# Moving the second chunk's recurrence into the next step, with shorter blocks and a new order, in an RWKV attention and feed-forward kernel

## What is computed

```python
xx = shift(x) - x;  lo = tanh((x + xx * maa_x) @ maa_w1.T) @ maa_w2      # four mixes
xrg, xwa, xk, xv = x + xx * (lo + time_maa)
r = xrg @ Wr.T;  k = xk @ Wk.T;  v = xv @ Wv.T;  g = tanh(xrg @ gate_w1.T) @ gate_w2
w = -softplus(-(time_decay + tanh(xwa @ decay_w1.T) @ decay_w2)) - 0.5
...                                    # kk (normalised), a, ma, mk, k, b = -kk * a
def step(s, inp):                      # per head, 32 x 32 state
    q_, w_, k_, v_, a_, b_ = inp
    sa = s @ a_
    s = s * exp(-exp(w_)) + outer(sa, b_) + outer(v_, k_)
    return s, s @ q_
y = head_norm(y) * ln_w + ln_b + rk * v
x = x + (y * g) @ Wo.T
x = x + quantised_matmul(layernorm(x), weight_q) + bias
```

## Time and profile before

| | before |
|---|---|
| median of three runs | 3132.63 us |
| the profiled execution | 3138.99 us, its span 3137.3 us |
| TensorE busy | 2873.8 us, 92% |
| VectorE busy | 2807.0 us, 89% |
| ScalarE busy | 1672.6 us, 53% |
| GpSimd busy | 1420.0 us, 45% |

### The profile page before, as it was taken

One profiled execution on the slowest core, in us unless ns is written; L12 is line 12 of the kernel. 1 busy time (PEld: TensorE's weight loads), 2 busy tenths in 40 slices (PEclk: granted clock), 3 DMA queues, 4 the chain that ended last, 5 costly groups with the idle time before them and its releaser, 6 DMA issues.

```text
span 3137.3 us, 175510 instructions
## 1 busy us (share of the span) xinstructions
PE 2873.8 (92%) x80064; PEld 2523.7 (80%) x80128; DVE 2807.0 (89%) x5699; ACT 1672.6 (53%) x3334; POOL 1420.0 (45%) x1224
## 2 busy tenths in 40 slices
PE   5899999999999999999999999999999999999995
PEld 5788788888887887888888888888888888888874
DVE  4898899999999998999999999999999899889985
ACT  3464555555554654655655655555555545546552
POOL 5344444444444444444444444444444444444442
PEclk9999999999999999999999999999999999999997
DMA  4121221222222222212212212212222222222121
GB/s 132 40 64 40 57 53 45 64 50 49 62 50 47 64 50 47 64 44 54 64 43 55 64 43 55 56 45 60 53 48 61 50 47 64 50 48 64 42 49 39
DMA packets 92603, 170.68 MB, mean 54 GB/s; under 512 B 13908, under 2 KB 14932, under 8 KB 91864
## 3 DMA queue, kind: packets, MB, share of 16 engines
q1 hardware_dynamic: 91864, 159.45, 21.7%
HBM read 41.97 MB, written 16.78 MB: 19 GB/s over the span
## 4 chain that ended last, share of the span: by engine, by line
PE 87%; DVE 7%; issue 5%; SPq 1%; DMA 0%; ACT 0%; POOL 0%; POOLq 0%; ACTq 0%; DVEq 0%
PE bank L1100 31%; PE bank_a L1239 12%; PE bank L1300 8%; PE bank L1107 4%; PE bank_a L1217 4%; PE bank_b L1217 4%; DVE stacked L939 4%; PE bank_a L1270 3%; PE bank_b L1270 3%; PE bank_a L1247 3%; PE bank_a L1255 3%; PE bank_b L1290 2%; PE bank_a L1290 2%; PE bank L1182 2%; DVE xm_k L816 2%
## 5 line engine op out<-in xcount | busy, mean ns | idle before, releaser
L1239 PE MATMUL bank_a<-pw,w_ffn_int 32*32 32x64 f32 x16384 | 273.0, 216 | 37.9 <-issue 33.2
L420 POOL TENSOR_TENSOR xm_wa<-xm_wa,xT 128x512 f32<-128x512 f32 x64 | 75.4, 1178 | 500.4 <-DVE xm_wa L816 500.4
L1239 PEld LDWEIGHTS bank_a<-pw,w_ffn_int 32*32 32x32 f32 x16384 | 242.3, 105 | 66.3 <-issue 53.2
L1100 PE MATMUL bank<-xm_rg,w_r 128*128 128x128 f32 x2048 | 285.7, 282 | 3.1 <-issue 3.1
L1100 PE MATMUL bank<-xm_v,w_v 128*128 128x128 f32 x2048 | 269.1, 279 | 4.6 <-issue 3.1
L527 ACT ACTIVATE pw<-bank_a 128x512 f32<-128x512 f32 x192 | 114.6, 597 | 287.2 <-PE bank_a L1239 286.7
L1100 PEld LDWEIGHTS bank<-xm_rg,w_r 128*128 128x128 f32 x2048 | 249.9, 192 | 15.4 <-issue 3.9
L1300 PE MATMUL bank<-w_o,yc 128*128 128x512 f32 x512 | 251.2, 614 | 11.3 <-DVE yc L781 10.3
L1100 PEld LDWEIGHTS bank<-xm_v,w_v 128*128 128x128 f32 x2048 | 245.1, 192 | 13.5 <-issue 7.7
L1100 PE MATMUL bank<-xm_k,w_k 128*128 128x128 f32 x2048 | 240.8, 276 | 2.0 <-issue 2.0
L1100 PEld LDWEIGHTS bank<-xm_k,w_k 128*128 128x128 f32 x2048 | 235.5, 193 | 2.2 <-issue 2.2
(11 more groups left out here) (198 smaller groups left out, 8334.3 us busy)
## 6 DMA issues: line engine op xcount, KB each, us to landing
streamed<-aq_state SPq DMA_DIRECT2D x128, 384.0 KB, 5.3
streamed<-w_ffn_int SPq DMA_DIRECT2D x128, 384.0 KB, 5.3
xin<-in_x SPq DMA_DIRECT2D x128, 128.0 KB, 4.8
xres<-in_x SPq DMA_DIRECT2D x128, 128.0 KB
out<-o_sb SPq DMA_DIRECT2D x128, 128.0 KB, 2.4
w_ffn_int<-in_weight_q SPq DMA_DIRECT2D x1, 2048.0 KB, 9.7
w_k<-in_Wk SPq DMA_DIRECT2D x1, 1024.0 KB
w_r<-in_Wr SPq DMA_DIRECT2D x1, 1024.0 KB
```

What stands on the lines that cost most here:

```text
L420: return nc.gpsimd.tensor_tensor(out_, in0, in1, ALU.add)
L1100: ins = mm(bank[:, o * n:(o + 1) * n], weights[:, k, o * P:(o + 1) * P], x[:, k].rearrange("p b t -> p (b t)"), start=(k == 0), stop=(k == ...
L1239: ins = mm(bank_a[q, 64 * n:64 * n + 64], pt[q, g, :], source[q, g, 0:2].rearrange("p j t -> p (j t)"), start=True, stop=True)
```

## The change

Four things change, and no matmul is added or removed.

The second chunk's from_values_and_state, solve_step, from_solutions, right_hand_sides, update_state, solution and outputs are called in the finish part of the next step, for tile n. Both chunks now use bank_b, so scores_k waits until both outputs of the tile before are read, and scores_b waits only for the inverse of the tile before. As scores_b of tile m is masked before chunk 1 of tile n is done, `first` becomes [P, 6, G, CHUNK], with two sets of the parts that from_solutions reads.

VectorE's and GpSimd's functions with several operations are split into functions with one (key_norm into squares_turned, squares_summed and squares_floored, and so on), and these are placed apart in tile_step.

VectorE's second product in scores_b (the crossing block) becomes an activation of ScalarE with mask_half as its scale, and VectorE's product for tx in half_inverse (the corner block) two activations. ScalarE's copy of the queries to r_raw goes: VectorE's queries_decayed reads the bank itself. gn_rstd is now yc's space in place of rn's.

All four orders of tile_step (TensorE, VectorE, ScalarE, GpSimd) are new; SP's stays.

```diff
+            def crossing(m):                                   # ScalarE
+                act.wait_ge(v_pm, count(m, 1, 1))
+                act.wait_ge(v_sums, count(m, POWERS, 0))
+                run(first[:, 1, :, 0:HALF], pairs(bank_a)[:, :, 0, HALF:], ACT.Identity,
+                    scale=mask_half[:, 0:1]).then_inc(a_e, 1)
+            def inverse_blocks(m):
+                act.wait_ge(v_t4, count(m, 1, 1))
+                act.wait_ge(p_u, count(m, NC, 0))
+                for a in range(2):
+                    c = slice(a * HALF, (a + 1) * HALF)
+                    ins = run(tx[:, :, c], pw[:, :, 1, HALF:], ACT.Identity, scale=mask_half[:, a * HALF:a * HALF + 1])
+                ins.then_inc(a_tx, 1)
...
-                dve.wait_ge(a_r, count(i, 1, 1))
-                tt(aq[:, 1], r_raw[:], pdec[:, :, 1:], ALU.mult).then_inc(v_q, 1)
+                tt(aq[:, 1], by_chunk(fb[2]), pdec[:, :, 1:], ALU.mult).then_inc(v_q, 1)
...
             def scores_b(m):                                   # TensorE
-                pe.wait_ge(a_y, count(m, NC, 0))
+                pe.wait_ge(v_t, count(m, 1, 0))
             def scores_k(m):
+                pe.wait_ge(a_y, count(m, NC, 0))
             def from_values_and_state(m, c):
-                bank = step_bank(c)
+                bank = bank_b
                 if c == 1:
-                    pe.wait_ge(v_t, count(m, 1, 1))
+                    pe.wait_ge(a_y, count(m, NC, 1))
```

More of the change, by code:

```diff
@@ L702, in tile_step @@
                     removal_pairs(m)
+                    key_pairs(m)
                 if project:
                     keys(i)
-                if solve:
-                    key_pairs(m)
+                if finish:
+                    solution(n, 1)
+                if project:
+                    a_gate(i)
+                    mk_gate(i)
+                if solve:
+                    crossing(m)
+                if project:
+                    decay_gate(i)
+                if finish:
+                    outputs(n, 1)
+                if project:
+                    ma_gate(i)
                 if finish:
                     squared_heads(n)
-                if project:
-                    a_gate(i)
-                    ma_gate(i)
-                if solve:
-                    value_pairs(m)
-                if project:
-                    mk_gate(i)
-                    squares(i)
                 if solve:
@@ L1284, in from_solutions @@
             def from_solutions(m, c):
-                bank = step_bank(c)
+                bank = bank_b
+                own = 2 + 2 * (m % 2)
                 if c == 0:
@@ L1322, in tile_step @@
                     keys(i, [0, 1])
+                if finish:
+                    from_values_and_state(n, 1)
+                if project:
                     keys(i, [2, 3])
+                if finish:
+                    solve_step(n, 1)
                 if solve:
@@ L1327, in tile_step @@
                     gates(i)
[L1328 to L1329 removed]
+                if finish:
+                    from_solutions(n, 1)
                 if project:
@@ L1340, in tile_step @@
                 if project:
-                    queries(i, [1])
-                    values(i, [2])
+                    values(i, [3])
+                if solve:
+                    scores_k(m)
+                if project:
                     queries(i, [2])
+                    queries(i, [3])
+                if solve:
+                    power(m, 2)
                 if mix:
@@ L1346, in tile_step @@
                 if solve:
-                    power(m, 2)
-                if project:
-                    queries(i, [3])
-                    values(i, [3])
+                    output_gate(m)
                 if finish:
@@ L1359, in tile_step @@
                 if solve:
-                    from_values_and_state(m, 0)
-                    inverse(m)
+                    half_inverse(m)
+                if project:
+                    gate_hidden(i)
                 if mix:
                     low_rank(j)
-                if project:
-                    gate_hidden(i)
                 if solve:
-                    solve_step(m, 0)
-                    output_gate(m)
-                    from_solutions(m, 0)
+                    from_values_and_state(m, 0)
                 if mix:
@@ L1372, in tile_step @@
                 if solve:
-                    from_values_and_state(m, 1)
-                if finish:
-                    quantised(n)
-                if solve:
-                    solve_step(m, 1)
-                if finish:
-                    feed_forward(n)
+                    inverse(m)
+                    solve_step(m, 0)
                 if mix:
@@ L1382, in tile_step @@
                 if solve:
-                    from_solutions(m, 1)
+                    from_solutions(m, 0)
+                if finish:
+                    quantised(n)
                 if mix:
                     hidden(j, 1)
+                if finish:
+                    feed_forward(n)
             pe.wait_ge(const_done, 1)
```

311 lines of the change are left out of this document (192 added, 119 removed).

## The result

The changed kernel is slower: 3259.39 us median (3247.39 to 3270.24) against 3135.11 us of the kernel before, run beside it; the ratio is 1.0384 [1.0358, 1.041]. The forecast was 3089 us with a range up to 3158. The profiled execution of after took 3247.39 us.

The account below looks back on a forecast made before the run. TensorE, with its waits, was taken to bound the 47.4 us step; -1.35 + 1.2 - 0.5 = -0.65 us a step, times 63 is -41, with the start -44: forecast 3089 us, range 3040 to 3158.

Parts of the forecast that it names:

- Second chunk's waits, -1.35: TensorE's waits at chunk 1's from_values_and_state, solve_step and feed_forward would go, covered by other matmuls: -1.35 us a step.
- Issue gaps elsewhere, -0.5: TensorE's unexplained stops in power and half_inverse would shrink as long matmul groups move apart: -0.5 us a step.
- The new wait, +1.2: solve_step(m,0) would wait +1.6 us a step for VectorE's xm_wa, xm_k, inverse; hidden issue gaps make it +1.2 net.
- the sign that the prediction had named: The prediction would be wrong if solve_step(m,0) waited over 2 us; 1.0 to 1.6 us was expected.
- a slack of 1.4 us: Time VectorE would have in hand each step to reach xm_wa before TensorE has filled the banks of mixed_inputs.
- 0.41 of issue gaps: The inverse's own issue gaps on TensorE, 0.41 us a step, would be free inside solve_step's new wait.
- Rival 3: VectorE late at xm_wa, lengthening solve_step(m,0)'s wait; decides from 0.65 us of lateness; slower, about 3183 us; chance 0.23.
- VectorE, 43.9 to 41.5: VectorE's work per step would fall from 43.9 to 41.5 us, by blocks leaving it and by splitting.
- The other 1.2, from the splitting: Separating about twelve dependent pairs of VectorE operations, gap about 0.1 us each, would save 1.2 us a step.

Follow-up runs that it names:

- norm_late: Changed kernel with only VectorE's second_norm and row_maximum moved behind inverse(m): 3182.5 us, ratio 1.0114 to the kernel before.
- gate_between: norm_late plus VectorE's inverse(m) between xm_wa and xm_k, ScalarE's value_pairs behind the table load, TensorE's gate_hidden(i) between inverse(m) and solve_step(m,0): 3100.88 us, ratio 0.9845.
- before_wait: Kernel before the change, with only VectorE's inverse(m) moved behind the quantiser so that solve_step(m,0) waits: 3215.35 us, ratio 1.0244.

## Why the prediction was wrong

*Second chunk's waits, -1.35.* Right. The waits of from_values_and_state, feed_forward and solve_step for rhs_sb fell from 86.2 us to about 4 (the last three rows of the list of waits): -1.28 a step.

*Issue gaps elsewhere, -0.5.* Right in size. The waits of before that answer to the list of after:

```profile
PE bank_a L1239 <- issue: 35.2, 48, 2.3
PE bank_a L1247 <- issue: 25.6, 37, 1.6
...
PE bank L1100 <- issue: 15.7, 18, 2.0
```

The issue gaps of power and half_inverse fell from 60.8 us to 23.3, which is -0.59; against it those of the projections rose from 15.7 to 24.0, +0.13. (The 63.7 of the prediction is all idle time of two rows and holds some waits for VectorE too.) That the spacing did it is argued from the order and wasn't tried alone.

*The new wait, +1.2.* This step failed first, and by the sign that the prediction had named: solve_step(m,0) waits over 2 us (2.13). The chain xm_wa, xm_k, inverse was read rightly: without the 0.58 us of lateness the wait in the step shown would be 1.33. But the sum took VectorE to be on time, on a slack of 1.4 us that wasn't there, and netted 0.41 of issue gaps that didn't shrink (36.2 us now). Wait and gaps of the inverse are 2.7 us a step together, where I had 1.6: 1.1 us too little. Rival 3 named the mechanism (VectorE late at xm_wa, by collisions with GpSimd and ScalarE's row ahead of power) and the point from which it decides, 0.65 us; by wait and gaps the lateness that reached TensorE was about 1.1 us. second_norm's stretch is 0.83 us of VectorE's delay ahead of xm_wa, its wait for GpSimd's rs another 0.43. I gave that rival 0.23 and 3183 us. Where the slack went stands in VectorE's own waits in after:

```profile
DVE rhs_sb L991 <- PE bank_b L1387: 92.5, 61, 1.9
DVE first L812 <- PE bank_a L1334: 86.5, 64, 2.0
DVE w_ffn_int L968 <- ACT pw L540: 85.9, 79, 4.3
...
DVE x2n L1055 <- POOL rs L477: 28.4, 63, 0.8
```

The prediction counted about 1 us a step each at scores_b's mask (L812) and at power(m,2) (L968, all three powers); they are 1.35 and 1.34. The waits at right_hand_sides (1.45) and for GpSimd's rs (0.44) it didn't count.

*VectorE, 43.9 to 41.5.* Wrong. Its busy time is 43.6 us a step. The crossing and the corner block did leave it (-1.22), but second_norm and scaled_rows took 0.83 and 0.50 more, and the small operation that makes `shift`, in norm_shift, 0.47 (172 to 644 ns each). The other 1.2, from the splitting, was too much to begin with: the earlier trace rows give 0.06 to 0.08 us a pair, not 0.1, and part of that is a gap, which busy time doesn't hold. That operations collide was right, but the earlier trace rows were misread: GpSimd's operation of 2.43 us starts 0.75 us behind values_centred and isn't the one that stretches it. A product of 1.31 us is, which starts at 1498.15, 0.50 us ahead: it runs on for 0.81 us, and values_centred takes 0.67 longer than its best. So the row speaks for a hold until the product ends, not against it. I didn't look for which operations would newly stand beside GpSimd's two-input products.

*What wasn't in the sum at all: the clock.* The forecast took TensorE's busy time to be constant. It rose by 81.7 us, 1.28 us a step. This is the larger half of the miss: norm_late has the wait that I forecast and still takes 3182.5 us. gate_between, where the wait is covered, takes 46.80 us a step: 0.64 less than before, where the sum had said 0.65. Part of that agreement is chance (its wait is gone, its issue gaps are larger), but it shows that the second chunk's move is worth what its waits were, once nothing takes their place.

The terms add up: -1.28 for the second chunk, +2.28 for wait and gaps at the inverse (2.69 less 0.41), about -0.5 for the other gaps, +1.28 of busy time make +1.8, against the measured +1.65.

## What to carry to other kernels

Price a new wait on TensorE not by its length alone: look at the granted clock behind it and at the duration of the same matmuls there, and count TensorE's busy time as something that a change can raise. Where a wait can't be removed, put work of the step over it, and first see to it that the other engine isn't the one that sets the pace, or the wait only starts earlier. When operations are moved, list for each operation of VectorE what GpSimd does at that time; a collision moved along the same path is not a gain.

## What the runs showed of the hardware

- Two added matmuls a step, at the place of the wait, took the ratio to before from 1.0384 to 1.0009, as the granted clock rose from 0.946 to 0.987. The same matmuls elsewhere took it to 1.077.
- A wait of about 1 us a step was enough for a granted clock of 0.955 in one order (norm_late) and left it at 0.982 in another (before_wait).
- A VectorE operation with one tensor input and two scalars per partition took 542 ns alone and 1367 ns beside a GpSimd product of 1.17 us.
- In single steps of the traces, VectorE operations that started beside a running GpSimd product lost most of what it still had to run: 0.67 of 0.81 us (values_centred in before), 0.85 of 1.11 (second_norm in after) and 0.55 of 0.70 (the operation of norm_shift in after, 0.71 us from 1515.19 against 0.16 in before, beside the product that ends at 1515.89).
